# ScalarE's square root and sigmoid change places in the first stage of a two-layer hybrid network

## The chip, the cores and the metric

The kernel runs on one core of a Trainium2 chip. The metric is the device time of one execution in microseconds. Engines are named as in the profile: PE is TensorE (PEld its weight loads), ACT is ScalarE, DVE is VectorE, POOL is GpSimd, SP is SyncE, which here only issues DMAs.

## What is computed

The reference is a chain of eight residual blocks over `x` of 8 x 512 x 256: delta rule attention, a butterfly feed-forward, distance attention, the same feed-forward, a long convolution, a mixture of low-rank experts, a state space layer, the same mixture. The edit is in the inputs of the first one:

```
x = layernorm(x)
q = l2_normalize(silu(x @ Wq.T).reshape(B, S, 16, 16))   # t / (norm(t) + 1e-6) over the last axis
k = l2_normalize(silu(x @ Wk.T).reshape(B, S, 16, 16))
v = silu(x @ Wv.T).reshape(B, S, 16, 16)
beta = sigmoid(x @ Wbeta.T)
for t in range(S):                                       # per batch and head
    out_t = q_t M
    M = M + beta_t * outer(k_t, v_t - M k_t)
```

## The kernel before, in words

All stages follow one another in one program, each a block in which every engine has its own instruction queue, written out by hand. Engines meet through semaphores: `then_inc` on an instruction, `wait_ge` in a queue. No planner orders the work; what stands in a queue's program is its order.

The first stage is `delta_inputs`. It works in `NB` = 8 turns, n = 0 to 7, and a turn covers four tiles of 128 tokens (512 rows). For each turn:

- POOL normalises the rows (`normalise`, L3095), two turns ahead. It also squares `q` and `k` (L3110), tile by tile, with two buffers in rotation.
- PE turns the rows (`turn_rows`, L2946), multiplies them with the weights of q and k (`queries_keys`, L2956, four tiles into three banks), of beta (`rates`, L2974) and of v (`values`, L2964). One turn behind, it transposes k, q and -beta*k (`turn_part`, L2994).
- ACT applies Silu to q and k out of PSUM (L3056), moves one half of the transposed parts (`put`, L3036), evicts the turned rows (`take_rows`, L3030), applies Silu to v (L3071), takes the square root of the sums of squares (L3074), applies Sigmoid for beta (L3078).
- DVE sums the squares (`squares`, L3130). One turn behind, it adds an epsilon to the roots (L3169), inverts them (L3171), scales q and k with four multiplications (L3176), makes -beta*k with four operations (L3183), and moves the other half of the transposed parts (`put`, L3124).
- SP stores the parts into DRAM for the next stage.

ACT's queue in turn n: the Silus of q and k of turn n, `put(n-1, K_)`, `put(n-1, Q_)`, `take_rows(n+1)` and the Silus of v in alternation, and then the two operations of the edit. In turn 0 the square roots of the layer norm's variances for the last three quarters of the tiles follow (`deviations(2)`, L3042); `deviations(0)` and `deviations(1)` stand right at the stage's start.

DVE's queue in turn n >= 1: in turn 1 first `scales(2)`, which waits for `deviations(2)`; then a wait for `root_done`, the add, the inversion, the four multiplications (`norm_done`), a wait for `beta_done`, the four operations for -beta*k (`nbk_done`), `put(o, K_, 1)`, `squares(n, 0)` and `(n, 1)`, `put(o, Q_, 1)`, `squares(n, 2)` and `(n, 3)`, `put(o, N_, 0)` and `(o, N_, 1)`, with o = n - 1. The turn n = 8 has only the part that is one behind.

PE's queue in turn n: `queries_keys(n, 0..3)`, of which the last waits for the first Silu of turn n, since there are three banks; `turn_part(n-1, K_)`, which waits for `norm_done`; `rates(n)`; `turn_part(n-1, Q_)`, whose second half writes the bank that DVE's `put(o, K_, 1)` must have emptied; `turn_rows(n+1, m)` and `values(n, m)` in alternation; `turn_part(n-1, N_)`.

ACT evaluates its functions from a table. Where the program has one function after another that the loaded table lacks, an `ACT_TABLE_LOAD` stands ahead of it in the compiled program; the kernel doesn't write these loads itself. Identity runs on whichever table is loaded.

After the stage come a barrier of all engines and the scan (`delta_scan`, 32 chunks of 16 tokens), in which ACT uses Identity, Square and Sqrt (L3602).

Of the kernel before, what the change touches and what calls it, by code (L numbers as in the profile page):

```python
# [6 lines left out]
ACT = mybir.ActivationFunctionType  # L7
# [14 lines left out]
class Core:  # L22
# [41 lines left out]
    def sem(self, name, ctx=None):  # L64

        handle = self.nc.alloc_semaphore(name)
        self.sems.append(handle)
        return handle
# [2767 lines left out]
def delta_inputs(nc, core, tag, x, ident, w_qk, w_vb, feat, tok_nbk, beside, cleared):  # L2836
# [4 lines left out]
    with ExitStack() as ctx:  # L2841
# [10 lines left out]
        ss = sbf("ss", [P, 2, 4 * 2 * NH])  # L2852
# [10 lines left out]
        sq_done, ss_done, root_done, inv_step = sem("sq_done"), sem("ss_done"), sem("root_done"), sem("inv_step")  # L2863
# [16 lines left out]
        def scale_parts(eng_op, part):  # L2880

            mean, var = (rows_of(core.mv[:, :, q], part) for q in range(2))
            return eng_op(rows_of(core.rstd[:], part), rows_of(core.shift[:], part), mean, var)

        def place(n, which, k):

            out = parts[which][:, n // 2 % 2, 2 * (n % 2):2 * (n % 2) + 2]
            return out.rearrange("p i c (b k) t -> p k i b c t", k=KD)[:, k]

        def columns(ps):  # L2890

            return ps.rearrange("p (i b c t) -> p i b c t", i=2, b=2, t=CT)
# [128 lines left out]
        @block.scalar  # L3021
        def _(act):
            a = nc.scalar.activation

            def take_rows(n, k):

                act.wait_ge(tr_done, KD * n + k + 1)
                if n >= 2:
                    act.wait_ge(v_ps, 2 * (n - 1))
                a(xnT[:, n % 2, k, :], psT[:, k, :], ACT.Identity).then_inc(xnT_done, 1)  # L3030

            def put(o, which):

                act.wait_ge(n_ps, 6 * o + 2 * which + 1)
                for i in range(2):
                    last = a(place(o, which, 0)[:, i], columns(psN[:, 0, :])[:, i], ACT.Identity)  # L3036
                last.then_inc(act_put, 1)

            def deviations(part):

                act.wait_ge(mean_done, part + 1)
                scale_parts(lambda rstd, shift, mean, var: a(rstd, var, ACT.Sqrt, bias=core.eps[:]),  # L3042
                            part).then_inc(deviation_done, 1)

            act.wait_ge(const_done, 2)
            deviations(0)
            deviations(1)
            for k in range(KD):
                take_rows(0, k)
            for n in range(NB + 1):  # L3050
                if n < NB:
                    if n >= 2:
                        act.wait_ge(n_ps, 6 * (n - 1))
                    for q in range(4):
                        act.wait_ge(a_ps, 4 * n + q + 1)
                        a(qk[:, n % 2, q, :], psA[:, q % 3, :], ACT.Silu).then_inc(silu_done, 1)  # L3056
                if n:
                    o = n - 1
                    if o % 2 == 0 and o // 2 >= 2:
                        act.wait_ge(stored[o // 2 % 2], 256 * (o // 4))  # L3060
                    put(o, K_)
                    put(o, Q_)
                if n < NB:
                    for m in range(KD):
                        if n + 1 < NB:
                            take_rows(n + 1, m)
                        act.wait_ge(v_ps, 2 * n + m + 1)
                        if n % 2 == 0 and n // 2 >= 2 and m == 0:
                            act.wait_ge(stored[n // 2 % 2], 256 * (n // 4))
                        for i in range(2):  # L3070
                            last = a(place(n, V_, m)[:, i], columns(psA[:, 1 + m, :])[:, i], ACT.Silu)  # L3071
                        last.then_inc(v_done, 1)
                    act.wait_ge(ss_done, 4 * n + 4)
                    a(ss[:, n % 2], ss[:, n % 2], ACT.Sqrt).then_inc(root_done, 1)  # L3074
                    act.wait_ge(b_ps, n + 1)
                    if n >= 2:
                        act.wait_ge(nbk_done, n - 1)
                    a(beta[:, n % 2], psB[:, 0:4 * NH].rearrange("p (j h) -> p j h", h=NH),  # L3078
                      ACT.Sigmoid).then_inc(beta_done, 1)
                    if n == 0:  # L3080
                        deviations(2)

# [802 lines left out]
```

## Time and profile before

| | us |
|---|---|
| median of 3 runs | 2493.41 |
| lowest, highest | 2484.53, 2494.43 |
| the profiled execution | 2493.41 |
| its span | 2491.6 |
| ACT_TABLE_LOAD, each | 1.283 |
| stage `delta_inputs`, up to the first instruction of the scan | 159.4 |

The span is the time between the first and the last instruction of the profiled execution; the execution's own time is a little longer. Rows of a timeline have the start and the duration in microseconds, then engine, line and operation; in square brackets stands the idle time of the engine just before and who ended it. Where a row has xN, N instructions in a row are merged. The granted clock is a share of TensorE's full speed.

### The profile page before, as it was taken

To read this page: it belongs to the slowest core of one execution; us is meant where nothing else is said; L and a number is where in the kernel's file an instruction comes from. 1 tells how busy PE (TensorE), PEld (TensorE's weight loads), DVE (VectorE), ACT (ScalarE), POOL (GpSimd) and SP (SyncE) were. 2 spreads that over 40 slices of the span, in tenths; PEclk is the share of its full clock that TensorE was granted. 3 is DMA by queue.
4 is the path that set the end of the run, shared out by engine and by line. 5 is a ranking of instruction groups with operands and counts; after the bars stand their busy time and mean duration, and the time that the engine had idled before them with its cause. 6 is when DMAs were issued, how large, how long until landed. Compare 5 with 4: busy or idle time off the path is not lost. (4 is left out here: it accounts for less than half of the span.)

```text
span 2491.6 us, 54329 instructions
## 1 busy us (share of the span) xinstructions
PE 2210.2 (89%) x21028; PEld 1618.1 (65%) x21028; DVE 1817.8 (73%) x4456; ACT 1406.8 (56%) x2165; POOL 1116.0 (45%) x1165
## 2 busy tenths in 40 slices
PE   7957777677899889999999988999898989999979
PEld 4645555565798745565666655998567856666669
DVE  6757777777666687888888855896674757767766
ACT  4632222222333279999999985555212567777755
POOL 4429999994101176678766852000351022233220
PEclk9979999999899989999999999999999999999999
DMA  5564545552100121122112211000001000000002
GB/s 180 169 188 138 150 131 146 160 162 68 61 1 14 41 67 59 54 67 74 54 59 65 65 44 38 1 1 1 15 1 40 1 1 1 1 1 1 1 1 69
DMA packets 158719, 148.87 MB, mean 60 GB/s; under 512 B 21440, under 2 KB 141376, under 8 KB 155392
## 3 DMA queue, kind: packets, MB, share of 16 engines
q1 hardware_dynamic: 138704, 105.51, 14.3%
q0 software_dynamic: 3456, 23.07, 2.8%
q10 hardware_dynamic: 16304, 16.83, 2.3%
q8 instruction: 168, 2.75, 0.5%
q14 instruction: 87, 0.71, 0.1%
HBM read 100.51 MB, written 40.63 MB: 57 GB/s over the span
## 5 line engine op out<-in xcount | busy, mean ns | idle before, releaser
L2057 DVE TENSOR_SCALAR_CACHE_REDUCE a_dist<-a_ring 128x512 f32<-128x512 f32 x512 | 336.5, 686 | 84.9 <-PE a_ring L1629 70.3
L2013 POOL TENSOR_SCALAR a_dist<-a_dist,a_mq 128x512 f32<-128x512 f32 x512 | 348.5, 701 | 67.2 <-ACT a_mq L1948 67.2
L1938 ACT ACTIVATE a_pT<-a_psT 128x1024 f32<-128x1024 f32 x256 | 257.7, 1024 | 58.6 <-PE a_psT L1641 40.8
L1641 PE MATMUL a_psT<-ident,a_dist 128*128 128x128 f32 x2048 | 273.1, 279 | 15.8 <-ACT a_pT L1938 12.6
L1641 PEld LDWEIGHTS a_psT<-ident,a_dist 128*128 128x128 f32 x2048 | 237.7, 143 | 57.0 <-issue 35.0
L1932 ACT ACTIVATE a_dist<-a_dist 128x2048 f32<-128x2048 f32 x128 | 236.0, 1901 | 15.4 <-DVE a_dist L2057 12.3
L3609 ACT ACTIVATE ds_wtm<-ds_wg,ds_par 128x256 f32<-128x256 f32 x64 | 29.1, 502 | 273.2 <-DVE ds_wg L3739 269.0
L1629 PE MATMUL a_ring<-a_stack 102*128 102x512 bf16 x512 | 175.4, 393 | 7.5 <-DVE a_dist L2057 6.3
L1258 POOL TENSOR_TENSOR c_y<-c_prod 128x1024 f32<-128x1024 f32 x16 | 39.2, 2472 | 294.5 <-DVE c_prod L1296 294.5
L1654 PE MATMUL a_psO<-a_pT,a_va 128*32 128x512 f32 x1024 | 133.7, 603 | 5.5 <-ACT a_pT L1938 5.5
L437 ACT ACTIVATE f_h<-a_psT,bf_bias_h 128x512 f32<-128x512 f32 x64 | 44.1, 690 | 128.0 <-PE a_psT L371 128.0
L2696 DVE SCALAR_TENSOR_TENSOR s_xbc<-s_padded,sw_cw,s_xbc 128x512 f32<-128x512 f32 x144 | 107.5, 748 | 8.3 <-ACT s_xbc L2556 4.7
L2670 POOL TENSOR_TENSOR s_xdec<-s_xdt,s_dv 128x512 f32<-128x512 f32 x24 | 25.0, 1042 | 197.5 <-ACT s_dv L2596 187.7
L1629 PEld LDWEIGHTS a_ring<-a_stack 102*128 102x128 bf16 x512 | 45.1, 99 | 101.6 <-DVE a_dist L2057 78.6
L2678 POOL TENSOR_TENSOR s_lt<-s_lt,s_gm 128x1024 f32<-128x1024 f32 x32 | 75.3, 2353 | 76.2 <-ACT s_lt L2606 76.2
L246 POOL TENSOR_TENSOR bf_t<-bf_up,bf_w 128x512 f32<-128x512 f32 x80 | 99.8, 1279 | 9.8 <-DMA bf_w<-in_up_w_dram 8.3
L2405 PE MATMUL s_psP<-s_xnT,sw_win 128*128 128x512 f32 x192 | 93.1, 618 | 9.7 <-ACT s_xnT L2548 6.0
L246 POOL TENSOR_TENSOR bf_t<-bf_down_t,bf_w 128x512 f32<-128x512 f32 x80 | 100.5, 1289 | 1.6
L1991 POOL TENSOR_TENSOR bf_up<-a_raw 128x512 f32<-128x512 f32 x28 | 32.8, 1172 | 149.4 <-DVE a_raw L2069 149.4
L480 DVE TENSOR_TENSOR f_h_lo<-f_h,f_h_hi 128x512 fp32r<-128x512 f32 x128 | 89.8, 702 | 4.4
L437 ACT ACTIVATE f_h<-f_psH,bf_bias_h 128x512 f32<-128x512 f32 x64 | 44.2, 690 | 70.2 <-PE f_psH L371 70.2
L478 DVE CAST f_h_hi<-f_h 128x512 fp32r<-128x512 f32 x128 | 56.1, 438 | 36.9 <-ACT f_h L437 36.6
(468 smaller groups left out, 6311.8 us busy)
## 6 DMA issues: line engine op xcount, KB each, us to landing
a_stack<-a_parts_dram SPq DMA_DIRECT2D x384, 64.0 KB
a_parts_dram<-a_parts SPq DMA_DIRECT2D x32, 384.0 KB, 2.4
bf_w<-in_up_w_dram POOLq DMA_DIRECT2D x10, 1024.0 KB, 8.4
bf_w<-in_down_w_dram POOLq DMA_DIRECT2D x10, 1024.0 KB, 7.0
ds_nbg<-tok_nbk ACTq DMA_DIRECT2D x128, 64.0 KB
feat_v<-di_part SPq DMA_DIRECT2D x16, 256.0 KB, 2.8
tok_nbk<-di_nbk SPq DMA_DIRECT2D x16, 256.0 KB, 2.8
feat_k<-di_part SPq DMA_DIRECT2D x16, 256.0 KB, 3.4
```

The lines of the kernel that those rows point to most:

```text
L246: e.tensor_tensor(t, v[:, :, i % 2, :], w, ALU.mult).then_inc(self.step, 1)
L437: gelu = lambda out: nc.scalar.activation(out, psH[m % 2], ACT.Gelu, bias=self.bf.bias_h[:, m:m + 1])
L480: tt(self.h_lo[:, m, :], self.h[:, n % self.RING, :], self.h_hi[:, m, :], ALU.subtract).then_inc(self.h_lo_done, 1)
L1629: mm(to[:], stack[0:NROW, u, 0, i, q * P:(q + 1) * P], stack[0:NROW, u, 1, i, :], start=True, stop=True).then_inc(ring_in, 1)
L1641: last = turn(psT[:, u % 2, kb, q * P:(q + 1) * P], dist[:, g % 2, i, q, k * P:(k + 1) * P], core.ident[:])
L1654: last = mm(psO[i * PAD:(i + 1) * PAD, :], va[:, par, kb, c:c + PAD], pT[:, i, kb // 2, kb % 2, :], start=(kb == 0), stop=(kb == TPB - 1))
L1932: a(dist[:, g % 2, i], dist[:, g % 2, i], ACT.Sqrt)
L1938: a(pT[:, u // 2, u % 2], psT[:, u % 2], ACT.Exp).then_inc(exp_done, 1)
L2013: last = nc.gpsimd.tensor_scalar(d, d, -1.0, mq[:, g % 2, i, q:q + 1], ALU.mult, ALU.add)
L2057: ts(dist[:, gg % 2, i, q, :], ps[:], 1e-12, 3.0e38, ALU.max, ALU.min, accum_out=mq[:, gg % 2, i, q:q + 1]).then_inc(ring_out, 1)
L2405: last = nc.tensor.matmul(out, lhsT, rhs, start=(k == 0), stop=(k == KD - 1))
L2696: last = stt(o, src[:, j:j + S], cw[:, c, j:j + 1], o, ALU.mult, ALU.add)
```

## The change

In ACT's queue, within each of the eight turns, Sqrt with its wait for the sums of squares now stands behind Sigmoid with its waits. Nothing else differs.

```
--- before.py
+++ after.py
@@ -3070,13 +3070,13 @@
                         for i in range(2):
                             last = a(place(n, V_, m)[:, i], columns(psA[:, 1 + m, :])[:, i], ACT.Silu)
                         last.then_inc(v_done, 1)
-                    act.wait_ge(ss_done, 4 * n + 4)
-                    a(ss[:, n % 2], ss[:, n % 2], ACT.Sqrt).then_inc(root_done, 1)
                     act.wait_ge(b_ps, n + 1)
                     if n >= 2:
                         act.wait_ge(nbk_done, n - 1)
                     a(beta[:, n % 2], psB[:, 0:4 * NH].rearrange("p (j h) -> p j h", h=NH),
                       ACT.Sigmoid).then_inc(beta_done, 1)
+                    act.wait_ge(ss_done, 4 * n + 4)
+                    a(ss[:, n % 2], ss[:, n % 2], ACT.Sqrt).then_inc(root_done, 1)
                     if n == 0:
                         deviations(2)
```

## Rows read from the trace of the kernel before

**Rows 1.** The page, busy time of each engine, share and instructions.

```profile
PE 2210.2 (89%) x21028; PEld 1618.1 (65%) x21028; DVE 1817.8 (73%) x4456; ACT 1406.8 (56%) x2165; POOL 1116.0 (45%) x1165
```

**Rows 2.** Windows: us, busy (instructions) of PE, PEld, DVE, ACT, POOL; clock, DMA.

```profile
100.00:120.00 20.00, 20.00 (x92) 11.87 (x90) 16.26 (x28) 13.47 (x26) 8.85 (x10) 1.00 0.49 147
...
146.00:150.00 4.00, 2.23 (x10) 1.87 (x11) 3.37 (x8) 0.66 (x2) 0.00 (x0) 0.50 0.21 67
```

**Rows 3.** Table loads on ACT: one line's view, then two groups.

```profile
L3074 ACT ACT_TABLE_LOAD  x8: 1283/1283/1283, 30.6 to 142.3; - x8
...
L3042 ACT ACT_TABLE_LOAD x2 | 2.6, 1283 | 6.9 <-DVE mv L3146 6.9
...
L2572 ACT ACT_TABLE_LOAD x8 | 10.3, 1283 | 0.1
```

**Rows 4.** Timeline, ACT, one steady turn.

```profile
49.63 1.28 ACT L3074 ACT_TABLE_LOAD   x1
...
51.25 1.28 ACT L3078 ACT_TABLE_LOAD   x1
52.55 0.22 ACT L3078 ACTIVATE di_beta<-di_psB 128x64 f32<-128x64 f32 x1
52.79 1.28 ACT L3056 ACT_TABLE_LOAD   x1
54.08 1.57 ACT L3056 ACTIVATE di_qk<-di_psA 128x512 f32<-128x512 f32 x3
...
65.23 1.28 ACT L3074 ACT_TABLE_LOAD   x1
```

**Rows 5.** Timeline, DVE, the same turn.

```profile
51.27 0.23 DVE L3169 TENSOR_SCALAR di_ss<-di_ss 128x128 f32<-128x128 f32 x1 [0.46 <-ACT di_ss L3074]
...
52.52 2.50 DVE L3176 TENSOR_TENSOR di_qk<-di_qk,di_ss 128x512 f32<-128x512 f32 x4
...
57.97 0.74 DVE L3124 COPY di_part<-di_psN 128x256 f32<-128x256 f32 x2
...
60.91 1.29 DVE L3130 TENSOR_REDUCE di_ss<-di_sqr 128x32 f32<-128x512 f32 x2
```

**Rows 6.** Timeline, DVE and PE, the turn at 35 to 45 us.

```profile
35.40 0.30 DVE L3152 RECIPROCAL rstd<-rstd 128x24 f32<-128x24 f32 x1 [9.09 <-ACT rstd L3042]
...
37.08 2.78 DVE L3176 TENSOR_TENSOR di_qk<-di_qk,di_ss 128x512 f32<-128x512 f32 x4
...
43.09 0.74 DVE L3124 COPY di_part<-di_psN 128x256 f32<-128x256 f32 x2
...
40.84 1.86 PE L2974 MATMUL di_psB<-di_wvb,di_xnT 128*128 128x16 f32 x16
...
44.44 0.60 PE L2946 MATMUL di_psT<-ident,di_xn 128*128 128x128 f32 x4
```

**Rows 7.** Timeline, PEld and PE, the steady turn.

```profile
54.73 0.30 PEld L2956 LDWEIGHTS di_psA<-di_wqk,di_xnT 128*128 128x128 f32 x2 [0.62 <-ACT di_qk L3056]
...
57.43 1.86 PE L2974 MATMUL di_psB<-di_wvb,di_xnT 128*128 128x16 f32 x16
...
60.04 0.60 PE L2946 MATMUL di_psT<-ident,di_xn 128*128 128x128 f32 x4
```

**Rows 8.** Timeline, PE, the stage's tail.

```profile
147.77 4.00 PE L2994 MATMUL di_psN<-ident,di_qk 128*128 128x128 f32 x16 [5.28 <-DVE di_qk L3176]
```

**Rows 9.** Timeline, ACT, first turn: start us, us, what, idle before.

```profile
33.75 1.28 ACT L3042 ACT_TABLE_LOAD   x1
```

**Rows 10.** A window of the scan, and starts of its chunks on DVE.

```profile
314.00:320.00 6.00, 5.40 (x108) 4.65 (x104) 3.86 (x15) 2.52 (x8) 5.84 (x6) 0.51 0.15 40
...
311.58 0.72 DVE L3753 STREAM_TRANSPOSE ds_bg<-ds_psB 128x512 f32<-128x512 f32 x1 [1.51 <-PE ds_psB L3486]
...
327.89 0.72 DVE L3753 STREAM_TRANSPOSE ds_bg<-ds_psB 128x512 f32<-128x512 f32 x1 [0.87 <-PE ds_psB L3486]
...
341.22 0.72 DVE L3753 STREAM_TRANSPOSE ds_bg<-ds_psB 128x512 f32<-128x512 f32 x1 [0.87 <-PE ds_psB L3486]
```

More of the change, by code:

```diff
@@ L3072, in _ @@
                         last.then_inc(v_done, 1)
-                    act.wait_ge(ss_done, 4 * n + 4)
-                    a(ss[:, n % 2], ss[:, n % 2], ACT.Sqrt).then_inc(root_done, 1)
                     act.wait_ge(b_ps, n + 1)
@@ L3079, in _ @@
                       ACT.Sigmoid).then_inc(beta_done, 1)
+                    act.wait_ge(ss_done, 4 * n + 4)
+                    a(ss[:, n % 2], ss[:, n % 2], ACT.Sqrt).then_inc(root_done, 1)
                     if n == 0:
```

## The prediction

> **What bounds the kernel now.** I begin with the page's totals [rows 1]: PE is busy for 89% of the span, but that is an average over a dozen stages. The edit touches ACT in the first stage alone, `delta_inputs`, so that stage has to be read by itself. The profiled execution lasted 2493.41 us for a span of 2491.6 us, so 1.8 us lie around the span, and it is also the median of the three runs (2484.53 to 2494.43). The sum below is made against 2493.41. Within 0.5% of that is 12.5 us, about what a measurement of this kernel can tell from no change.
>
> Next the windows [rows 2]. From 100 to 120 us, the steady part of the stage, PE is busy without a gap at a granted clock of 1.00. ACT is at 13.5 of 20 us, DVE at 16.3. A busy PE is not yet the bound, though; its time may be stretched by what it waits for. The table loads [rows 3] show why ACT matters: the row of L3074 (Sqrt) has eight loads of 1283 ns from 30.6 to 142.3 us, one for each turn. L3078 (Sigmoid) and L3056 (Silu) have a row like it each, so a turn has three, and the scales of the layer norm (L3042) have two more.
>
> The timeline of ACT [rows 4] shows one turn. After the last `v` eviction the Sqrt's load starts at 49.63, the Sigmoid's load at 51.25, the Sigmoid at 52.55, the Silu's load at 52.79, and the Silus of the next turn at 54.08. The next turn's load is at 65.23: a period of 15.60 us. PE's `queries_keys(n, 3)` waits for the first of these Silus. From there PE works without a pause to the last `values`, whose eviction starts the next trio of loads. So the cycle that sets the period runs through all three loads, and the edit keeps its length unless the number of loads changes.
>
> DVE runs beside this cycle [rows 5]: root ready, add at 51.27, reciprocal, four multiplications that end at 55.02, four `nbk` operations, and the copy `put(o, K_, 1)`, which ends at 57.97 + 0.74 = 58.71. PE needs it twice: `turn_part(o, K_)` waits for the multiplications, the second half of `turn_part(o, Q_)` for the copy.
>
> **The change, part by part.** Sqrt and Sigmoid change places, with their waits. No arithmetic and no DMA is added.
>
> *The order.* Each of the two is a load and a short operation. Sigmoid's pair takes 52.79 - 51.25 = 1.54 us, Sqrt's pair 51.25 - 49.63 = 1.62 us [rows 4]. If the loads stay, Silu starts where it did, the root is ready 1.54 us later and `beta` 1.62 us earlier. The early `beta` is worth nothing: DVE wants it only after its four multiplications (at 55.02 for a `beta` done at 52.77). The late root holds up DVE, which had only just begun to wait for it (0.46 us of idle time at L3169).
>
> *What the late root costs in one turn.* I take PE's shortest distance from the turn at 37 to 45 us, where DVE really holds it up [rows 6], and compare it with the steady turn [rows 7].
> For `turn_part(o, K_)`: in the held turn `rates` (L2974) starts at 40.84, 0.98 us after the multiplications' end at 37.08 + 2.78 = 39.86. In the steady turn it starts at 57.43, 2.41 us after 55.02. Slack 1.43 us, so 1.54 us more delays PE by 0.11.
> For `turn_part(o, Q_)`: in the held turn `turn_rows` (L2946) starts at 44.44, 0.61 us after the copy's end at 43.83. In the steady turn it starts at 60.04, 1.33 us after 58.71. Slack 0.72 us, so PE is late by 1.54 - 0.72 = 0.82 us. That includes the 0.11. What is late next: `values`, its eviction, and with it the next trio of loads. The cycle now runs through DVE, and each turn grows from 15.60 to 16.42.
> Of the eight trios the first starts at 30.6 and the last at 142.3 [rows 3]; the second is the one at 49.63. Six intervals of this form lie between the second and the eighth: 6 x 0.82 = +4.92 us. Bounds for this term: 0 (all covered) and 6 x 1.54 = 9.2 (no slack at all). I take the middle value, since both distances are read from the same instructions. Queued behind DVE's late copy are the squares' reductions, and behind those POOL's third and fourth product; the last reduction now ends at 60.91 + 1.29 = 62.20, and the Sqrt's load that follows its wait starts at 65.23 and itself moves later, so this wait stays covered.
>
> *The tail.* After the last turn nothing hides the root. PE sits idle for 5.28 us until the multiplications that follow the last root are done (147.77) [rows 8], and the stage's end and its stores hang on it. The root 1.54 us later: +1.54 us.
>
> *The first turn.* There `deviations(2)`, a Sqrt too, follows. Before, the order is Sqrt, Sigmoid, Sqrt, with a load each; that of `deviations(2)` starts at 33.75 and takes 1.28 us [rows 9]. After, it is Sigmoid, Sqrt, Sqrt, and the last needs no load; the two `deviations` at the start ran on one load in the same way (`deviations` is called three times, L3042 has two loads, [rows 3]). A load and the step to its operation are 1.29 us (51.25 to 52.55 is 1.30). DVE waits for exactly this operation: `scales(2)` stands before the roots in its queue, and its idle time of 9.09 us ends there [rows 6]. So -1.29 us, passed on in full through DVE's multiplications to PE. Bounds: 0 and -1.29.
>
> *The last load.* Sqrt's table now stands at the end of the stage, so the one load of L3602 in the scan (at 287 us) may go. It lies beside DVE's solve, whose end DVE waits for anyway: nothing gained. Were it on the path it would be 1.28 us once.
>
> Sum: -1.29 + 4.92 + 1.54 = +5.17 us, thus 2493.41 + 5.17 = 2498.6 us. That is +0.2%, below what can be told from no change. With the bounds of the terms the sum lies between +0.3 and +10.8.
>
> **Does Sigmoid keep its load?** This decides the sign. The rows say that after Sigmoid the Silu needed a load [rows 3, 4], so the table loaded for Sigmoid doesn't hold Silu. They don't say whether the table loaded for Silu holds Sigmoid; in the kernel before, a Sqrt always stood between. By the Trainium skill (ScalarE activation tables: per-element evaluation and per-set limits, section Table sets in the compiler and the runtime) loads are placed by the greedy longest run; by that rule a table with both would have been chosen at Sigmoid and no load would stand at Silu, so there is none with both, and the time is 2498.6 us. The trace speaks against the rule in another place: Exp, Ln and Exp at L2570, L2572 and L2596 have eight loads each (the row of L2572 stands for the three, [rows 3]), though the skill (ScalarE: Activation LUTs, section Table sets: the hidden batching unit) names a set with both. So the placement may be simpler than the rule, and the rival below stays.
>
> The price of a load is 1.28 us, plus 0.01 us to the next operation [rows 4]. The skill (ScalarE: Activation LUTs, section What ACT_TABLE_LOAD costs) gives about 2.66 us for a switch, with the drain; the trace doesn't agree, for the load at 51.25 and the Sigmoid at 52.55 are 1.30 apart. By the page's figure the first turn's term would be an estimated -2.7 instead of -1.29.
>
> **The rivals.**
> *Silu's table holds Sigmoid (faster, though little).* Then each turn loses a load. Sigmoid runs at once, and Sqrt's load starts 0.24 us later than before (52.55 to 52.79, [rows 4]). Silu starts 1.29 us earlier. PE's weight load waits 0.62 us for the Silu in a steady turn [rows 7], and can gain at most that. DVE's copy comes 0.24 later against a slack of 0.72, so 0.72 - 0.24 = 0.48 us are gained: 6 x 0.48 = 2.9. First turn: two loads, 2.6, less what PE isn't ready for, say 2.3. Tail: +0.24. Sum -5.0: 2488.4 us.
> *The late root is covered.* If PE has more slack than the two distances show, the steady term is 0: -1.29 + 1.54 = +0.25, 2493.7 us. For it speaks that PE is never idle in the steady part; against it, that 0.72 is less than 1.54 by more than any rounding.
> *TensorE's clock (slower).* At 146 to 150 us, after the idle time of the tail, the granted clock is 0.50, the lower of the two levels, 1.2 GHz [rows 2]. In the scan it falls again here and there: at 314 to 320 it is 0.51 [rows 10]. The chunk of the scan across that dip takes 16.31 us (311.58 to 327.89), the next one 13.33 (to 341.22), so one dip costs 3.0 us. A shifted or longer idle time could bring more such dips. It decides from (12.5 - 5.2) / 3.0 = 2.4, thus three more dips than now: 2498.6 + 9 = 2507.6 us. Against it: the new idle times of PE in the steady part are at most 0.82 us, and the long idle time ahead of the low clock is there already.
>
> **How the numbers follow.** Loads stay and DVE is late: 0.65, 2498.6 us, its own range 2493 to 2504 (dips more or fewer, bounds of the terms). Silu's table holds Sigmoid: 0.18. Late root covered: 0.09. Clock: 0.08. Predicted is the likeliest, 2498.6. The range reaches over the first three, from 2486 (the fast rival less a bit of the runs' spread) to 2504. All but the clock stay within 12.5 us of 2493.41; for faster by over 0.5% the fast rival must meet three dips fewer: 0.03. Slower: the clock, 0.07. Same: 0.90.
>
> **What would show it.** Right: the trios on ACT as Sigmoid's load, Sqrt's load, Silu's load; L3042 with one load; the trios' period 16.4 us; DVE's idle time before L3169 about 2 us; `turn_rows` on PE with an idle time near 0.7 us; the tail's idle time of PE 6.8 us instead of 5.28. L3078 without its loads would mean the first rival; a period still at 15.60 with loads unchanged the second; more slices of low clock in the scan the third. The prediction is wrong if the stage's end moves by more than 10 us either way, or if later stages, which do the same work, don't take over the shift.

## The result, and the profile after

The changed kernel takes 2506.18 us (median of 6 runs, 2498.80 to 2515.93) beside 2491.99 us for the kernel before (6 runs): a ratio of 1.0061, interval 1.0033 to 1.0091. A second comparison (experiment 7) gave 2506.66 beside 2490.02 us, ratio 1.0068, interval 1.0045 to 1.0091. So it is slower by 14 to 17 us, and not by 5. A ratio here is estimated from all runs and is not the quotient of the two medians; the two can differ by up to 0.2%. The profiled execution of the changed kernel took 2502.61 us, its span is 2500.8 us, 9.2 us more than before.

The timeline of ACT in the changed kernel, one steady turn (it answers to [rows 4]), with the operation of `deviations(2)` from turn 0 ahead:

```profile
32.93 0.31 ACT L3042 ACTIVATE rstd<-mv,eps 128x24 f32<-128x24 f32 x1
...
69.90 1.28 ACT L3076 ACT_TABLE_LOAD   x1
71.19 0.22 ACT L3076 ACTIVATE di_beta<-di_psB 128x64 f32<-128x64 f32 x1
71.43 1.28 ACT L3079 ACT_TABLE_LOAD   x1
72.73 0.31 ACT L3079 ACTIVATE di_ss<-di_ss 128x128 f32<-128x128 f32 x1
73.05 1.28 ACT L3056 ACT_TABLE_LOAD   x1
74.35 1.57 ACT L3056 ACTIVATE di_qk<-di_psA 128x512 f32<-128x512 f32 x3
...
87.29 1.28 ACT L3076 ACT_TABLE_LOAD   x1
```

Sigmoid keeps its load. All three stand there, Silu starts 4.45 us after the trio begins, as before, and `deviations(2)` runs without a load of its own. But the period is 87.29 - 69.90 = 17.39 us, where 15.60 was before and 16.42 was forecast.

The timeline of DVE in the same turn (as [rows 5]):

```profile
73.07 0.23 DVE L3169 TENSOR_SCALAR di_ss<-di_ss 128x128 f32<-128x128 f32 x1 [2.00 <-ACT di_ss L3079]
...
74.31 4.19 DVE L3176 TENSOR_TENSOR di_qk<-di_qk,di_ss 128x512 f32<-128x512 f32 x4
78.53 1.43 DVE L3183 SCALAR_TENSOR_TENSOR di_nbk<-di_qk,di_beta 128x256 f32<-128x256 f32 x4
79.88 0.74 DVE L3124 COPY di_part<-di_psN 128x256 f32<-128x256 f32 x2
```

The idle time ahead of the add is 2.00 us instead of 0.46: the root is 1.54 us late, as worked out. What was not worked out is the second row shown. The four multiplications take 4.19 us instead of 2.50, and the four `nbk` operations behind them 1.43 instead of 3.00. POOL's timeline says why; here the first two products of this turn in the changed kernel:

```profile
75.03 2.92 POOL L3110 TENSOR_TENSOR di_sqr<-di_qk 128x512 f32<-128x512 f32 x2 [5.28 <-ACT di_qk L3056]
```

and these are the rows of the kernel before that I had not weighed, POOL's products in the steady turn, then DVE's `nbk` operations (those of L3183, which make -beta*k) in that turn and in the tail, where POOL runs no product:

```profile
54.76 2.33 POOL L3110 TENSOR_TENSOR di_sqr<-di_qk 128x512 f32<-128x512 f32 x2 [5.29 <-ACT di_qk L3056]
```

```profile
55.05 3.00 DVE L3183 SCALAR_TENSOR_TENSOR di_nbk<-di_qk,di_beta 128x256 f32<-128x256 f32 x4
...
147.75 1.43 DVE L3183 SCALAR_TENSOR_TENSOR di_nbk<-di_qk,di_beta 128x256 f32<-128x256 f32 x4
```

Before, POOL's products (54.76 to 57.09) lay beside the `nbk` operations (55.05 to 58.05), which took twice as long as in the tail. The multiplications had ended at 55.02, just ahead. In the changed kernel the products start at the same place in ACT's cycle, 5.13 us after the trio begins, but the multiplications now last until after that. PE's timeline in the changed kernel (as [rows 7, 8]) shows who pays:

```profile
78.56 1.09 PE L2994 MATMUL di_psN<-ident,di_qk 128*128 128x128 f32 x8 [1.57 <-DVE di_qk L3176]
79.48 1.86 PE L2974 MATMUL di_psB<-di_wvb,di_xnT 128*128 128x16 f32 x16
...
82.10 0.60 PE L2946 MATMUL di_psT<-ident,di_xn 128*128 128x128 f32 x4
...
162.94 3.99 PE L2994 MATMUL di_psN<-ident,di_qk 128*128 128x128 f32 x16 [6.81 <-DVE di_qk L3176]
```

PE waits for the multiplications, not for DVE's copy `put(o, K_, 1)`. They end 1.54 + 1.68 = 3.22 us later in the cycle, against the slack of 1.43 us that the prediction read for this wait: 1.79 us, and 15.60 + 1.79 = 17.39.

The windows of the changed kernel show one more thing that the kernel before has not (columns as in [rows 2]):

```profile
40.00:44.00 4.00, 3.20 (x19) 2.64 (x19) 4.00 (x9) 1.10 (x3) 1.98 (x3) 0.77 0.41 117
...
60.00:64.00 4.00, 4.00 (x20) 4.00 (x20) 1.48 (x4) 0.66 (x2) 2.04 (x2) 0.50 0.83 250
...
100.00:120.00 20.00, 18.43 (x83) 10.86 (x83) 13.63 (x26) 11.64 (x23) 8.20 (x10) 1.00 0.57 169
```

PE's granted clock falls to the lower level (1.2 GHz) within the stage. The interval across the second such stretch is 69.90 - 49.19 = 20.71 us instead of 17.39. Before, the clock was 1.00 from 20 to 140 us.

The first instruction of the scan shows where the stage ends, before and then changed:

```profile
159.43 1.80 POOL L3401 MEMSET ds_nbx<- 128x2048 f32 x1 [16.52 <-POOLq L2841]
```

```profile
173.91 1.80 POOL L3401 MEMSET ds_nbx<- 128x2048 f32 x1 [17.50 <-POOLq L2841]
```

That is 14.5 us later, and 15.2 us later counted from the first trio's start (30.60 before, 29.89 here), which the edit cannot have moved.

By its terms the stage loses 11.0 us through its waits (-1.29 + 6 x 1.79 + 1.54) and in this execution about 5 us through the clock (19.30 instead of the 17.6 that experiment 3 has for the first interval, and 20.71 instead of 17.39). That makes 16.0, 0.8 more than the 15.2 read at its end. How the later stages pass it on can be read at two lines. First the kernel before, then the changed one; the columns are the durations, then the first and the last start:

```profile
L101 ACT ACTIVATE rstd<-mv,eps x2: 322/322/323, 647.1 to 1745.2; 128x32 f32<-128x32 f32 x2
...
L130 ACT ACTIVATE rstd<-mv,eps x8: 282/292/323, 1530.3 to 2424.5; 128x28 f32<-128x28 f32 x4, 128x4 f32<-128x4 f32 x4
```

```profile
L101 ACT ACTIVATE rstd<-mv,eps x2: 322/322/323, 660.4 to 1754.1; 128x32 f32<-128x32 f32 x2
...
L130 ACT ACTIVATE rstd<-mv,eps x8: 280/293/324, 1539.1 to 2433.7; 128x28 f32<-128x28 f32 x4, 128x4 f32<-128x4 f32 x4
```

+13.3 us just behind the scan, +8.8 at 1530 us. The work between is the same, and one execution there differs from another by some microseconds (experiment 3 ends the stage 2.1 us before the kernel before and passes L101 6.6 us before it), so a single pair of spans (+9.2) says less than the medians.

### The profile page after: what moved, and what is told of

The parts are those of the page before. It is cut to its first block and busy times, and to the rows that moved or that the text cites. A ratio compares the mean times of both kernels' runs of the same rounds, so it can differ in the third digit from the quotient of the medians.

```text
span 2500.8 us, 54327 instructions
## 1 busy us (share of the span) xinstructions
PE 2211.0 (88%) x21028; PEld 1618.1 (65%) x21028; DVE 1817.7 (73%) x4456; ACT 1406.0 (56%) x2163; POOL 1121.3 (45%) x1165
## 5 line engine op out<-in xcount | busy, mean ns | idle before, releaser
L1932 ACT ACTIVATE a_dist<-a_dist 128x2048 f32<-128x2048 f32 x128 | 236.0, 1901 | 14.5 <-DVE a_dist L2057 11.3
```

The source lines that it names most:

```text
L1932: a(dist[:, g % 2, i], dist[:, g % 2, i], ACT.Sqrt)
```

## The experiments

All times are medians in us beside the kernel before on the same chip; experiments 1 to 4 share one set of its runs, 5 to 8 another, 9 to 11 a third. The fifth column has the experiment's median and then that of the kernel before. All start from the changed kernel, except 4, which starts from the kernel before.

| kernel | period, us | PE waits in each turn, us | clock below 1.00 from 50 to 140 us | median, before | ratio, interval |
|---|---|---|---|---|---|
| before | 15.60 | 0 | no | | |
| changed | 17.39 | 1.57 | yes | 2506.18, 2491.99 | 1.0061, 1.0033 to 1.0091 |
| 1 products behind the multiplications | 16.54 | 0.64 | yes | 2499.42, 2493.49 | 1.0027, 1.0009 to 1.0046 |
| 2 products behind nbk | 15.70 | 0 | no | 2489.51, 2493.49 | 1.0001, 0.9980 to 1.0021 |
| 3 change in turn 0 only | 15.60 | 0 | no | 2490.82, 2493.49 | 0.9998, 0.9981 to 1.0015 |
| 4 more products, order of before | 16.69 | 0.88 | yes | 2502.96, 2493.49 | 1.0036, 1.0013 to 1.0058 |
| 5 ten matmuls in PE's wait | 17.82 | filled | no | 2516.51, 2490.02 | 1.0095, 1.0064 to 1.0126 |
| 6 Silu for beta | 15.97 | 0.21 | no | 2495.94, 2490.02 | 1.0016, 0.9995 to 1.0037 |
| 7 changed again | 17.39 | 1.57 | yes | 2506.66, 2490.02 | 1.0068, 1.0045 to 1.0091 |
| 8 turn 0 and products behind nbk | 15.60 | 0 | no | 2491.40, 2490.02 | 1.0000, 0.9984 to 1.0016 |
| 9 six matmuls in PE's wait | 17.39 | 0.24 left | no | 2505.00, 2492.18 | 1.0044, 1.0025 to 1.0063 |
| 10 ten matmuls again | 17.82 | filled | no | 2518.71, 2492.18 | 1.0107, 1.0083 to 1.0130 |
| 11 turn 7 as before | 17.39 | 1.57 | yes | 2507.37, 2492.18 | 1.0060, 1.0036 to 1.0083 |

The period is that of a turn with the clock at 1.00. The fourth column is of one profiled execution each.

**1. POOL's products behind the multiplications.**

```
                     pool.wait_ge(silu_done, 4 * n + q + 1)
+                    if n and q == 0:
+                        pool.wait_ge(norm_done, 4 * n)
```

> The changed kernel, with POOL's first product of each turn (n >= 1) held until DVE's four multiplications are done, so that they never overlap. Theory A (the late root moved DVE's multiplications under POOL's products: 4.18 us for four instead of 2.50, and that costs PE 1.79 us a turn): the four take 2.5 us again, the four nbk operations 3.0 as in the kernel before, PE waits for the copy instead, and the period between ACT's trios falls from 17.39 to about 16.4 us; the whole kernel is near 5 us above the kernel before. Theory B (the late root by itself costs 1.79 us, whoever runs beside): the period stays at 17.4 us and the kernel 11 to 14 us above.

DVE's timeline of this kernel:

```profile
69.97 2.50 DVE L3178 TENSOR_TENSOR di_qk<-di_qk,di_ss 128x512 f32<-128x512 f32 x4
72.50 3.12 DVE L3185 SCALAR_TENSOR_TENSOR di_nbk<-di_qk,di_beta 128x256 f32<-128x256 f32 x4
75.54 0.74 DVE L3126 COPY di_part<-di_psN 128x256 f32<-128x256 f32 x2
```

and PE's, ahead of the second half of `turn_part(o, Q_)` one turn earlier:

```profile
59.89 0.63 PE L2994 MATMUL di_psN<-ident,di_qk 128*128 128x128 f32 x4 [0.64 <-DVE di_part L3126]
```

The root is as late as in the changed kernel, yet the multiplications take 2.50 us and the period is 16.54 us. PE waits for the copy: this is the turn that the prediction described, 0.12 us longer because `nbk` takes 3.12. Theory B is refuted. The whole is 5.9 us above the kernel before by the medians, near the 5 expected; this trace has three stretches of low clock in the stage besides, 1.7 us each.

**2. POOL's products behind nbk.** The same edit with `pool.wait_ge(nbk_done, n)`.

> The changed kernel, with POOL's first product of each turn held until the four nbk operations are done too. Theory A: neither group of DVE is slowed (2.5 and 1.4 us), the root that is 1.54 us late is made up for by the 1.57 us that nbk saves, the period is about 15.7 us, the kernel within 1 or 2 us of the kernel before. Theory B: 17.4 us and 11 to 14 us above.

```profile
66.22 2.50 DVE L3178 TENSOR_TENSOR di_qk<-di_qk,di_ss 128x512 f32<-128x512 f32 x4
68.75 1.43 DVE L3185 SCALAR_TENSOR_TENSOR di_nbk<-di_qk,di_beta 128x256 f32<-128x256 f32 x4
```

Both groups run at their own speed, the period is 15.70 us, and the whole is level with the kernel before (1.0001). One wait on POOL takes the whole loss away with the late root still there; POOL's products start later for it, but PE has no wait in these turns.

**3. The change in turn 0 only.**

```
+                    if not (n == 0):
+                        act.wait_ge(ss_done, 4 * n + 4)
+                        a(ss[:, n % 2], ss[:, n % 2], ACT.Sqrt).then_inc(root_done, 1)
                     act.wait_ge(b_ps, n + 1)
...
+                    if n == 0:
+                        act.wait_ge(ss_done, 4 * n + 4)
+                        a(ss[:, n % 2], ss[:, n % 2], ACT.Sqrt).then_inc(root_done, 1)
```

> Only turn 0 has the Sqrt behind the Sigmoid; the others are as before. Both theories: one table load fewer, the second trio of loads 1.3 us earlier after the first (17.7 us instead of 19.03), the period 15.60, the whole 1.3 us below the kernel before, which a timing can't tell from no change. A third theory, that the time comes from the lower granted clock in the stage rather than from the order of the turns, would have low clock in the stage here too.

The first interval is 48.26 - 30.64 = 17.62 us instead of 19.03, the others 15.60. The saved load is worth 1.4 us in that interval, and the timing can't show so little (0.9998, 0.9981 to 1.0015). Theory A and B say the same here; the third theory, low clock whatever the order of the turns, finds no low clock.

**4. More products on POOL, in the order of before.**

```
+                    if n and q == 0:
+                        pool.wait_ge(inv_step, 2 * n)
+                        pool.wait_ge(xn_done, 4 * min(n + 2, NB))
+                        for i in range(2):
+                            t = xn[:, 2 * i:2 * i + 2, :].rearrange("p a d -> p (a d)")
+                            nc.gpsimd.tensor_tensor(sqr[:, i, :], t, t, ALU.mult).then_inc(idle_done, 1)
+                        pool.wait_ge(idle_done, 2 * n)
                     pool.wait_ge(silu_done, 4 * n + q + 1)
```

(`idle_done` is a semaphore of its own.)

> The kernel before, in its own order, with two more products on POOL in each turn n >= 1, started when DVE's reciprocal is done, so that they run beside the four multiplications (their results are not used). Theory A: the root is on time, and still the four multiplications take about 4.2 us instead of 2.5; the copy ends 1.7 us later against a slack of 0.72, the period is about 16.5 us, the whole near 6 us above the kernel before. Theory B: 2.5 us and a period of 15.60.

DVE and then POOL in one turn of this kernel:

```profile
74.59 5.03 DVE L3184 TENSOR_TENSOR di_qk<-di_qk,di_ss 128x512 f32<-128x512 f32 x4
79.65 2.15 DVE L3191 SCALAR_TENSOR_TENSOR di_nbk<-di_qk,di_beta 128x256 f32<-128x256 f32 x4
```

```profile
74.64 2.98 POOL L3113 TENSOR_TENSOR di_sqr<-di_xn 128x512 f32<-128x512 f32 x2 [3.10 <-DVE di_ss L3179]
77.70 2.82 POOL L3118 TENSOR_TENSOR di_sqr<-di_qk 128x512 f32<-128x512 f32 x2
```

ACT's order is untouched and the root on time, and the multiplications double. The size was off, 5.03 instead of 4.2, since the turn's own products followed at once and met them too; the period came out at 16.69 (16.5 expected). The whole is 9.5 us above the kernel before by the medians, where near 6 was expected; this trace has three stretches of low clock.

**5, 9 and 10. PE's wait filled.** Matmuls of the identity, ten, six, and ten again:

```
+                if n and n < NB:
+                    if n > 1:
+                        pe.wait_ge(dve_put, 4 * (n - 2) + 3)
+                    core.keep_busy(psN[:, 0, :], 10)
                 if n:
                     turn_part(n - 1, K_)
```

> The changed kernel, with ten matmuls of the identity on PE ahead of the transposes of k in each turn from 1 to 7, where PE otherwise waits 1.57 us for DVE's multiplications. They write a bank that the transposes overwrite, and work off no wait. Theory C (PE's idle time in each turn also brings stretches of low granted clock in the stage, which cost the part of the 14 us above the 11 that the waits explain): the period stays at 17.4 us, but the stage has no slice below 1.00 between 20 and 140 us, and the median is near 11 us above the kernel before. If low clock is there by chance, it comes here as well, and the median is the changed kernel's, 14 us above.

> As the kernel with ten matmuls in PE's idle time, but six: 1.4 us against an idle time of 1.57, so that they no longer lengthen the turn. Theory C (idle time of PE in each turn brings the low clock of the stage, and filling it takes that away): period 17.4 us, no slice below 1.00 between 20 and 140 us, the median near 11 us above the kernel before instead of 14 to 16. If the filling brings low clock somewhere else instead, which the median of the ten matmuls (26 us above) points to, the stage is clean again but the median stays at 14 us or more, with less clock in the scan after it.

> The kernel with ten matmuls in PE's idle time once more. Its first profiled execution was its fastest (2502 us) and its median 2516.5, so the trace did not show where the time went. The turns explain 14 us above the kernel before (period 17.82). If the 26 us were drawn by chance, the median is near 2504 now; if they are real, it is near 2516 again, and a profiled execution that is slow shows the slices of low clock that make it so.

The window of the kernel with six, over all the turns:

```profile
20.00:150.00 130.00, 127.41 (x613) 80.48 (x611) 88.98 (x184) 74.59 (x139) 54.06 (x56) 1.00 0.48 146
```

With the wait filled the clock stays at 1.00 through all turns, in all three traces. The last trio of the kernel with six begins at 151.31 us, that of the changed kernel at 155.97 and 159.53 in its two traces. The stage ends at 169.24 us in it, 9.8 us after the kernel before, against 14.5 and 18.0 us in the changed kernel's two traces. The whole shows this less well: by the medians it is 12.8 us above the kernel before and by the ratio 11.0, where 11 was expected and the changed kernel has 14 to 17; the intervals overlap. With ten the turn is 0.43 us too long (17.82, where experiment 5 expected 17.4), which makes some 14 us, and 26 were measured twice. In the second trace of that kernel the shift against the kernel before is 10.7 us at L101 (657.8), 10.6 us at L130 (1540.9) and 20.6 us at the end of the span (2512.2), and in the trace of the kernel with six it is 3.3 us (650.4), 3.1 us (1533.4) and 13.5 us (2505.1). So some 10 us of each arise in late stages that none of these edits touches, and there the granted clock falls. Here the same window in the kernel before, with six and with ten matmuls (experiment 10):

```profile
2300.00:2480.00 180.00, 163.29 (x1052) 132.17 (x1051) 125.15 (x280) 115.55 (x242) 33.88 (x21) 1.00 0.06 18
```

```profile
2300.00:2480.00 180.00, 164.21 (x963) 129.92 (x961) 120.74 (x268) 112.46 (x238) 35.74 (x22) 0.94 0.04 13
```

```profile
2300.00:2480.00 180.00, 164.17 (x948) 127.99 (x947) 121.32 (x263) 113.29 (x241) 41.38 (x26) 0.94 0.03 10
```

In the other eleven traces it is 1.00, but for 0.98 in experiment 1. Experiment 5, the same kernel as 10, is among them, but its profiled execution was the fastest of its six. Whether the filling brings this late low clock, as the rival in the expectation of experiment 9 has it for the scan, or whether it came by chance, stays open.

**6. Silu in place of Sigmoid for beta.**

```
-                      ACT.Sigmoid).then_inc(beta_done, 1)
+                      ACT.Silu).then_inc(beta_done, 1)
```

> The changed kernel with Silu in place of Sigmoid for beta (so beta is another number); the table of Silu is loaded already, so this is the changed kernel as it would be if one table held both. Theory A: one load fewer in each turn, the root only 0.24 us later than before the change, but POOL's products start 1.3 us earlier and meet the multiplications again (about 4.2 us for four), so the period is about 16.1 us. Without a collision (the rival in the prediction) it is 15.1 us. The whole by theory A is about 1 us above the kernel before, by the rival 5 us below.

```profile
64.11 0.23 DVE L3169 TENSOR_SCALAR di_ss<-di_ss 128x128 f32<-128x128 f32 x1 [0.57 <-ACT di_ss L3079]
...
65.36 4.18 DVE L3176 TENSOR_TENSOR di_qk<-di_qk,di_ss 128x512 f32<-128x512 f32 x4
```

Two loads a turn, the root on time, and the multiplications still take 4.18 us, since Silu and with it POOL's products come 1.3 us sooner. The period is 15.97 (16.1 expected, 15.1 by the rival). Had one table held both, the forecast of 2488.4 us for that case, 5.0 us below the kernel before, would have been wrong as well: the medians stand 5.9 us above it and the ratio 4.0 us (interval -1.2 to +9.2), where about 1 was expected. The stage does not show that much: it ends at 157.85 us, 1.6 us before that of the kernel before, so the rest arises behind it.

**7. The changed kernel again.**

> The changed kernel once more, for a second look at the granted clock of the stage and at how far the median stands above the kernel before. Theory A: all waits and durations as in the first trace, period 17.39 us. Theory C: slices of low clock between 20 and 140 us again. By chance only: as likely none.

The same turn in this second trace, and three stretches of low clock (40 to 48, 56 to 68, 80 to 88 us) instead of two. The interval across the third is 90.84 - 70.14 = 20.70 us, 3.3 more than the period, as across the second (70.14 - 49.42 = 20.72). With 19.31 instead of 17.62 for the first interval the clock costs 8.3 us here, and the stage ends at 177.47 us.

**8. Turn 0 as changed, the others as before, products behind nbk.** The edits of 2 and 3 together.

> The version that the runs so far point to: Sqrt behind Sigmoid in turn 0 only, and POOL's first product of each turn held until DVE's nbk operations are done. Theory A: one load fewer, no collision in any turn: the first interval between the trios about 16.6 us instead of 19.03, the period 15.60 (ACT's loads bound it now), the tail as before; about 2.4 us below the kernel before, too little for a timing to tell from no change.

The trace has what was expected: first interval 46.04 - 29.41 = 16.63, period 15.60, PE never waits. The stage ends at 155.13 us, 3.1 us less than in the kernel before counted from the first trio (2.4 expected). The timing shows no gain (1.0000, 0.9984 to 1.0016), and could not be sure to show one so small. The period is that of the kernel before, so more slack on DVE buys nothing.

**11. Turn 7 as before.** The edit of experiment 3 with `n < NB - 1` in place of `n == 0`.

> The changed kernel with turn 7 in the order of before. All theories: the stage's tail is as before, PE idle 5.28 us in it instead of 6.81, and the whole 1.54 us below the changed kernel, thus some 9.5 us of waits above the kernel before and 12 to 14 in all.

```profile
161.68 3.97 PE L2994 MATMUL di_psN<-ident,di_qk 128*128 128x128 f32 x16 [5.28 <-DVE di_qk L3180]
```

The tail's wait is 5.28 us again, 1.53 less than 6.81. From the first trio's start to the stage's end it is 142.50 us (30.15 to 172.65) against 144.02 in the first trace of the changed kernel (29.89 to 173.91), which has the same stretches of low clock, so the 1.5 us are passed on. The whole can't show so little: 15.2 us above the kernel before by the medians, where 12 to 14 was expected.

## Why the prediction was wrong, point by point

- **Bound of the stage.** Right: the cycle of the turns ran through ACT's three loads, with DVE beside it, and later through DVE.
- **The order, root 1.54 us late, beta worthless.** Right: idle time ahead of the add 2.00 us instead of 0.46.
- **What the late root costs in one turn.** This is the step that failed. It moved DVE's multiplications by 1.54 us and kept their duration of 2.50 us. The new place lies beside POOL's products, and they took 4.18. Both slacks were right (1.43 and 0.72 us): experiment 1, with no collision there, gives the forecast turn, 16.54 against 16.42. With 3.22 us instead of 1.54 the first wait decides: 1.79 us instead of 0.82, six times, 10.7 instead of 4.9 us. The bound of 9.2 us for this term assumed fixed durations too and was too low, and with it the upper end of the sum, +10.8 us. The rows of the kernel before would have told it: `nbk` at 3.00 us beside POOL and at 1.43 in the tail. The Trainium skill has the rule (SBUF — State Buffer, section Who interferes with whom): a DVE instruction with two inputs in SBUF contends with a GpSimd instruction that reads SBUF, and issue order decides who waits. The traces agree that these two kinds slow each other, with the numbers above; where the two groups lie side by side both lose, DVE 1.68 us and POOL 0.89 (2.93 instead of 2.04 for two products).
- **The tail.** Right: 6.81 us of idle time instead of 5.28, and experiment 11 takes 1.5 us back at the stage's end.
- **The first turn.** Right: one load fewer; the interval is 17.62 us instead of 19.03 in experiment 3. In the changed kernel it is 19.30, because a stretch of low clock fell into it.
- **The last load.** Right: L3602 has no load in the changed kernel, and experiment 11, which ends its turns on Sigmoid, has it.
- **Does Sigmoid keep its load.** Right, it does, and the first rival falls. Experiment 6 shows moreover that the rival's time was worked out with the same mistake. Which rule places the loads was not tried.
- **The late root is covered.** Refuted: even with the products kept off the multiplications (experiment 1) PE still waits 0.64 us and the period is 16.54, not 15.60.
- **TensorE's clock.** The mechanism was named, at the wrong place and with the wrong point of decision: I set PE's new idle time at 0.82 us a turn and took that for harmless. The waits are 1.57 us, and the five kernels and traces with 0.64 us or more in each turn (changed twice, 1, 4, 11) have low clock between 50 and 140 us, while the other eight (before, 2, 3, 5, 6, 8, 9, 10) have none; in these PE's wait is nil, 0.21 us, or filled with matmuls, down to 0.24 us with six. As filling the wait took it away three times of three, I count the wait as its cause there. The stretch at 40 to 48 us (up to 52 in experiment 4) is another matter. It stands in the same five traces and in none of the other eight, but it begins ahead of the first of these waits, and experiment 3, whose turns up to there are the changed kernel's, lacks it; why it falls where it does stays open. What the clock costs, 5.0 us in the first trace (1.7 and 3.3), 8.3 in the second and 3 to 6 between the medians and the 11 us of waits, rests on intervals of single traces and on medians whose own intervals are as wide. That this rival's 2507.6 us lies so near the measured 2506.18 is luck: it had 4.9 us for the late root and 9 for low clock in the scan, and the runs show 10.7 us for the late root and the low clock within the stage.
- **The sign of being wrong.** It was a move of the stage's end by more than 10 us, and it came: 14.5 and 18.0 us in the two traces.

Sum as measured: -1.3 + 10.7 + 1.5 = +11 us by waits, and 3 to 6 us that the low clock of the stage explains in size, against +14 and +17 in the two comparisons.

## What to carry to other kernels

When an edit moves an instruction in time, its duration is not a constant: look at what the other engines run at the new place (here POOL, beside DVE's instructions with two inputs in SBUF), and read the same instruction where it runs alone and where it doesn't. One line whose instructions take 3.00 us in one place and 1.43 in another is such a sign. And a wait put on the engine that has slack (here POOL) can take back what a reordering on another engine has cost; here it took back all of it.

## What the runs showed of the hardware that I had not expected

- Four DVE multiplications of 128x512 f32 with both inputs in SBUF: 2.50 us alone, 4.18 us beside two POOL products of the same shape, 5.03 us beside four. Four `nbk` operations of 128x256: 1.43 us alone, 3.00 to 3.12 us beside two. Two POOL products: 2.04 us alone, 2.33 to 2.40 beside `nbk`, 2.93 beside the multiplications.
- A wait of PE as short as 0.64 us, but in every turn, went with stretches of the lower clock, each worth 1.7 us (18.22 instead of 16.54 in experiment 1) to 3.3 us of a turn; the waits of the kernel before in its turn at 35 to 45 us (2.30, 0.60 and 0.80 us), which come in that one turn only, did not.
- A table stays loaded from one block of the program into the next: the first Sqrt of the scan, 150 us later, needed no load once the stage before ended on Sqrt.
